# The last round of a fused attention and expert kernel: sums loaded and made earlier, a bias added by TensorE, a gate product made ahead, mixes put between the scores, and four stores of one tile each

## The reference, cut to what matters

```python
xn = layernorm(x)
q, k, v = (xn @ W + b).reshape(b, s, 4, 256)        # 4 heads
scores = (q*cos . k*cos + q*sin . k*sin) / 16        # [b, s, head, head] at every position
out = softmax(scores) @ v                            # mixes the 4 heads of one position
s_ = swapaxes(out, 1, 2).reshape(b, s, 4*256) @ Wo + bo
# experts: 8, two of them for every position, gates from a Sinkhorn router
e = sum over the 2 chosen of gate * ((relu(xn @ wg) * (xn @ wp)) @ wo)
result = x + s_ * silu(xn + e)
```

## Time and profile before

| | |
|---|---|
| median of 3 runs | 1723.53 us (1723.3 to 1725.36) |
| the profiled execution's own time | 1719.48 us |
| its span | 1717.7 us |
| TensorE busy | 95% of the span |
| GpSimd busy | 46% of the span |
| mean granted TensorE clock | 0.985 of full |

### The profile page before, as it was taken

The page is one execution under the profiler, slowest core; times in us unless marked ns, Lnnn a source line. Parts: engine busy times, 40 slices in busy tenths (PEclk is TensorE's granted clock), DMA queues, the critical chain, the costliest instruction groups (busy, mean ns, idle before and its releaser), DMA issues.

```text
span 1717.7 us, 28581 instructions
## 1 busy us (share of the span) xinstructions
PE 1638.2 (95%) x9328; PEld 1271.6 (74%) x9328; DVE 994.2 (58%) x1895; ACT 734.5 (43%) x1207; POOL 792.1 (46%) x961
## 2 busy tenths in 40 slices
PE   4899899989999999999999999999999999999994
PEld 2446766678888888888888887776687767877663
DVE  6567889853333333333333335667777677776775
ACT  3666333413333333333333335345554455543551
POOL 4665378713433333343434432525545455452435
PEclk9999999999999999999999999999999999999997
DMA  9997633163313131313111412444546445455234
GB/s 332 401 360 245 248 123 104 51 249 127 126 53 124 56 123 56 124 55 123 56 56 56 153 54 85 152 138 160 169 154 214 137 159 171 154 178 172 91 122 131
DMA packets 161574, 250.96 MB, mean 146 GB/s; under 512 B 13864, under 2 KB 121184, under 8 KB 160288
## 3 DMA queue, kind: packets, MB, share of 16 engines
q1 hardware_dynamic: 147968, 213.57, 35.8%
q0 software_dynamic: 12960, 35.41, 6.3%
q10 hardware_dynamic: 512, 0.16, 0.0%
HBM read 149.58 MB, written 99.50 MB: 145 GB/s over the span
## 4 chain that ended last, share of the span: by engine, by line
PE 84%; DMA 5%; DVE 4%; SPq 2%; ACT 2%; POOL 2%; issue 1%; ACTq 0%; POOLq 0%; DVEq 0%
PE ps L1075 20%; PE ps L1012 20%; PE ps L1023 13%; PE ps L967 12%; PE ps L1094 10%; PE ps L1084 3%; DMA AUX<-xn_d,AUX 3%; PE ps L981 2%; PE ps L1057 2%; DVE UN L1159 1%; PE ps L922 1%; PE ps L866 1%; SPq L323 1%; DMA WR<-w_d 1%; SPq L304 1%
## 5 line engine op out<-in xcount | busy, mean ns | idle before, releaser
L1075 PE MATMUL ps<-WR,FR 128*128 x1620 | 409.8, 402 | 5.2 <-issue 2.7
L1075 PEld LDWEIGHTS ps<-WR,FR 128*128 128x128 f32 x1620 | 297.5, 190 | 64.6 <-issue 6.8
L603 POOL DMA_INDIRECT y_d<-AUX x135 | 133.3, 987 | 368.2 <-ACT AUX L810 368.2
L1574 DVE TENSOR_TENSOR AUX<-AUX,ps 128x512 f32<-128x512 f32 x135 | 92.9, 688 | 348.2 <-ACT AUX L798 348.2
L760 ACT ACTIVATE WM<-ps,bcs,trig 128x512 f32<-128x512 f32 x256 | 255.7, 1019 | 90.2 <-PE ps L1012 82.4
L1510 DVE TENSOR_SCALAR WM<-ps,vec,trig 128x512 f32<-128x512 f32 x256 | 246.4, 995 | 63.9 <-ACT WM L760 63.5
L967 PEld LDWEIGHTS ps<-WM 128*128 128x128 f32 x2048 | 230.6, 192 | 9.0 <-issue 5.8
L1023 PE MATMUL ps<-WM,XTJ 128*128 128x512 f32 x512 | 237.1, 600 | 0.0
L967 PE MATMUL ps<-WM 128*128 128x128 f32 x2048 | 234.6, 276 | 2.0 <-DVE TM L1406 2.0
L798 ACT ACTIVATE AUX<-ps 128x512 f32<-128x512 f32 x135 | 80.9, 599 | 324.5 <-PE ps L1075 324.5
L1012 PE MATMUL ps<-XH,WH 128*128 128x512 f32 x512 | 205.1, 401 | 6.5 <-issue 5.5
(11 more groups left out here) (234 smaller groups left out, 2218.9 us busy)
## 6 DMA issues: line engine op xcount, KB each, us to landing
u_d<-UN SPq DMA_DIRECT2D x128, 256.0 KB, 2.0
US<-u_d SPq DMA_DIRECT2D x64, 512.0 KB, 4.7
WR<-w_d SPq DMA_DIRECT2D x8, 3072.0 KB, 10.9
AUX<-y_d SPq DMA_DIRECT2D x30, 512.0 KB, 5.9
WM<-in_L_attn_x_dram SPq DMA_DIRECT2D x16, 512.0 KB, 9.3
xn_d<-WM SPq DMA_DIRECT2D x32, 256.0 KB, 8.7
w_d<-WH SPq DMA_DIRECT2D x16, 512.0 KB, 8.4
w_d<-WL SPq DMA_DIRECT2D x16, 512.0 KB, 9.4
```

Of the source, the lines that this page charges most:

```text
L603: e.indirect_dma_start(y_d, bass.IndirectOffsetOnAxis(toks[:, m - 5:m - 4], 0), YS[:, (m - 5) % 2, :], None).then_inc(s_y[(m - 5) % 2], 16)
L1075: mm = e.matmul(b[:, :], x, WR[:, bass.ds(off[m] + (2048 * z + 1024 * a + 512 * k), 512)], start=(k == 0 and x is xh and z == 0), stop=(k ...
L1574: e.tensor_tensor(HS[:, m % 2, :], GR[:, :], mP[m % 2][:, :], ALU.mult).then_inc(s_h, 1)
```

## The change

- `load_c(15)` is issued at the end of round 14's part of the SyncE queue, right behind `load_c(14)`, into other tiles (cE1 to cE3, which the totals of rounds 0 to 3 used, and AB for x), with a semaphore of its own. The U of item 63 goes to XB and waits for no mix.
- On GpSimd `total(15)` stands ahead of `finish(14)`. ScalarE's `silu(15)` stands behind group 23 of round 15. A new function `ahead` on GpSimd, behind `finish(14)`, makes gate times bo (into xn's tile) and adds x to it (4 x 2 operations).
- The mix of items 60 to 63 no longer waits for VectorE's bias: TensorE adds BR with four more matmuls a mix. `mixed` of these items makes `PSUM * gate` and then adds what `ahead` made, and so takes in `result`.
- Mix 60 stands behind the scores of item 62, mix 61 behind the scores of item 63; on VectorE each item's spread stands behind the next item's soft_a.
- `store_last` stores each item with one DMA as soon as it is ready.

```diff
@@ cs, us
-            return [M_s[:, i // 2, 2048 * (i % 2):2048 * (i % 2) + 1024].rearrange("p (i d) -> p i d", d=D)
-                    for i in range(4)]
+            return cE1, cE2, cE3, AB[:, :, :].rearrange("p a (i d) -> p (a i) d", d=D)
+        ends = cs(NQ - 1)
+        def us(n):
+            return XB[:, :, :] if n == 4 * NQ - 1 else US[:, n % 3, :, :]
@@ SyncE
+            def store_last(n):
+
+                e.wait_ge(s_rl, n - 4 * NQ + 5)
+                e.dma_start(rows(of, NQ - 1)[:, :, n % 4, :].rearrange("h r d -> r h d"),
+                            cs(NQ - 1)[3][:, n % 4, :]).then_inc(s_o, 16)
@@ SyncE, segment
+                    if q == NQ - 2:
+                        e.wait_ge(s_es, 64 * QE)
+                        load_c(NQ - 1)
                 if q1 == NQ:
-                    e.wait_ge(s_ch, 24 * NQ)
-                    load_c(NQ - 1)
                     load_u(4 * NQ - 1)
...
-            store_c(NQ - 1)
+            for n in range(4 * NQ - 4, 4 * NQ):
+                store_last(n)
@@ GpSimd
+            def ahead():
+
+                _, y2, xn, xx = cs(NQ - 1)
+                e.wait_ge(s_cg, NQ - QE)
+                for i in range(4):
+                    ch(e.tensor_tensor(xn[:, i, :], y2[:, i, :], bo_b[:, :], ALU.mult))
+                    e.tensor_tensor(xx[:, i, :], xn[:, i, :], xx[:, i, :], ALU.add).then_inc(s_z, 1)
...
-                if q > QE:
+                if QE < q < NQ:
                     total(q - 1)
                 if q in host:
                     total(host[q])
-                if q > QE:
+                if q == NQ - 1:
+                    total(q)
+                if QE < q < NQ:
                     finish(q - 1)
+                if q == NQ - 1:
+                    ahead()
@@ ScalarE, segment
+                        if q == NQ - 1 and c == 23:
+                            silu(q)
...
-                if q1 == NQ:
-                    silu(NQ - 1)
@@ TensorE, mix
                 for c in range(4):
-                    mm = e.matmul(pM(n)[32 * c:32 * c + 32, :],
-                                  AT[:, n % 2, 32 * c:32 * c + 32], US[:, n % 3, c, :], start=True, stop=True)
+                    at = AT[:, n % 2, 32 * c:32 * c + 32]
+                    last = n < 4 * NQ - 4
+                    mm = e.matmul(pM(n)[32 * c:32 * c + 32, :], at, us(n)[:, c, :], start=True, stop=last)
+                    if not last:
+                        mm = e.matmul(pM(n)[32 * c:32 * c + 32, :], at, BR[:, :], start=False, stop=True)
@@ VectorE, mixed
+                i = n % 4
+                _, y2, _, xx = ends
+                e.wait_ge(s_z, i + 1)
+                e.tensor_tensor(ro(n), pM(n), y2[:, i, :], ALU.mult).then_inc(s_pm, 1)
+                e.wait_ge(s_pm, n + 1)
+                e.tensor_tensor(xx[:, i, :], ro(n), xx[:, i, :], ALU.add).then_inc(s_rl, 1)
@@ VectorE, segment
                         if i:
                             soft_b(n - 1)
+                        if q == NQ - 1 and i:
+                            spread(n - 1)
+                            if i == 3:
+                                mixed(n - 3)
...
-                spread(n)
-                biased(n)
-                spread(n + 1)
-                biased(n + 1)
-                for i in range(4):
-                    mixed(n + i)
-                    if i < 2:
-                        spread(n + i + 2)
-                        biased(n + i + 2)
+                if q1 == NQ:
+                    spread(4 * NQ - 1)
+                    for i in range(1, 4):
+                        mixed(4 * NQ - 4 + i)
```

More of the change, by code:

```diff
@@ L226, in program @@
         s_o = sem("s_o")
-        s_sa2, s_pm = sem("s_sa2"), sem("s_pm")
+        s_sa2, s_pm, s_u63, s_c15, s_z, s_rl = (
+            sem(n) for n in ("s_sa2", "s_pm", "s_u63", "s_c15", "s_z", "s_rl"))
         block = ctx.enter_context(nc.Block())
@@ L365, in load_u @@
                     e.wait_ge(s_uw[i], 16 * ((w - i + 2) // 3))
-                if n >= 3:
+                if n == 4 * NQ - 1:
+                    e.wait_ge(s_xt, 2 * NQ)
+                elif n >= 3:
                     e.wait_ge(s_mx, n - 2)
-                e.dma_start(US[:, n % 3, :, :], u_in[n]).then_inc(s_us[n % 3], 16)
+                e.dma_start(us(n), u_in[n]).then_inc(s_u63 if n == 4 * NQ - 1 else s_us[n % 3], 16)
             def store_r(n):
@@ L379, in store_c @@
                     e.dma_start(rows(of, q)[h], cs(q)[3][h:128:4]).then_inc(s_o, 16)
+            def store_last(n):
+                e.wait_ge(s_rl, n - 4 * NQ + 5)
+                e.dma_start(rows(of, NQ - 1)[:, :, n % 4, :].rearrange("h r d -> r h d"),
+                            cs(NQ - 1)[3][:, n % 4, :]).then_inc(s_o, 16)
             def load_c(q):
                 y1, y2, xn, xx = cs(q)
-                e.dma_start(y1, blk(y_d, q)).then_inc(s_cl, 16)
-                e.dma_start(y2, blk(y_d[N:2 * N, :], q)).then_inc(s_cl, 16)
-                e.dma_start(xn, blk(xn_d, q)).then_inc(s_cl, 16)
+                sl = s_cl if q < NQ - 1 else s_c15
+                e.dma_start(y1, blk(y_d, q)).then_inc(sl, 16)
+                e.dma_start(y2, blk(y_d[N:2 * N, :], q)).then_inc(sl, 16)
+                e.dma_start(xn, blk(xn_d, q)).then_inc(sl, 16)
                 if QE < q < NQ - 1:
@@ L389, in load_c @@
                 for h in range(H):
-                    e.dma_start(xx[h:128:4], rows(xf, q)[h]).then_inc(s_cl, 16)
+                    e.dma_start(xx[h:128:4], rows(xf, q)[h]).then_inc(sl, 16)
             def load_e(k):
@@ L610, in total @@
                 else:
-                    e.wait_ge(s_cl, 112 * (q - QE + 1))
+                    e.wait_ge(*((s_cl, 112 * (q - QE + 1)) if q < NQ - 1 else (s_c15, 112)))
                     y1, y2, xn, _ = cs(q)
@@ L974, in mix @@
                 e.wait_ge(s_atc, n + 1)
-                e.wait_ge(s_ub, n + 1)
+                if n < 4 * NQ - 4:
+                    e.wait_ge(s_ub, n + 1)
+                elif n == 4 * NQ - 1:
+                    e.wait_ge(s_u63, 16)
+                else:
+                    e.wait_ge(s_us[n % 3], 16 * (n // 3 + 1))
                 if n == 0:
@@ L1039, in segment @@
                         scores(4 * q + i)
+                        if q == NQ - 1 and i >= 2:
+                            mix(4 * q + i - 2)
                         place(lists.get((q, 24 + i), ()))
                 if q1 == NQ:
-                    for i in range(4):
-                        mix(4 * q1 - 4 + i)
+                    mix(4 * NQ - 2)
+                    mix(4 * NQ - 1)
             e.wait_ge(s_wsp, 4)
@@ L1453, in mixed @@
                     e.wait_ge(s_ro, n - 4 * QE - 3)
-                e.tensor_tensor(ro(n), pM(n), bo_b[:, :], ALU.add).then_inc(s_pm, 1)
+                if n < 4 * NQ - 4:
+                    e.tensor_tensor(ro(n), pM(n), bo_b[:, :], ALU.add).then_inc(s_pm, 1)
+                    return
+                i = n % 4
[4 more added lines that the diff above has]
+                e.tensor_tensor(xx[:, i, :], ro(n), xx[:, i, :], ALU.add).then_inc(s_rl, 1)
             def early(k):
@@ L1537, in segment @@
                     soft_b(4 * q + 3)
-                if q1 == QE:
-                    return
-                n = 4 * q1 - 4
-                spread(n)
-                biased(n)
-                spread(n + 1)
-                biased(n + 1)
-                for i in range(4):
-                    mixed(n + i)
-                    if i < 2:
-                        spread(n + i + 2)
-                        biased(n + i + 2)
+                if q1 == NQ:
+                    spread(4 * NQ - 1)
+                    for i in range(1, 4):
+                        mixed(4 * NQ - 4 + i)
             segment(0, QE)
```

## The result

The changed kernel took 1713.41 us in the median of 11 runs (1707.27 to 1718.27), the kernel before 1723.53 (1719.94 to 1728.47, 11 runs). The ratio is 0.9925, with a 95% interval of 0.9909 to 0.9942: faster by 0.75%, 10 to 16 us. That ratio is not the quotient of the two medians: they lie 10.1 us apart (0.9941), at the low end of the interval. Its profiled execution took 1709.11 us with a span of 1707.4, so 10.3 us less span than before.

A forecast was written before the change was run, and what follows sets the result against it. TensorE bounds the rounds; behind the last scores, 27.3 us of load, GpSimd total, silu, result and store. Leaving VectorE's chain and mixes there cuts the span from 1717.7 to 1704.4, giving a 1710.2 us median, range 1708.6 to 1714.5.

The forecast's parts named there:

- What bounds the end: Behind the scores: 27.3 us on load, GpSimd's total, silu, result, store; VectorE's chain ends only 4.5 us earlier.
- The early load and total cost nothing: Rounds 14 and 15: load lands about 1651, second total ends about 1663, TensorE's rounds stay at 53.7 us.
- a rival of up to 1 us: Ahead of mix 56: moved totals slow VectorE, TensorE waits up to 1 us; chance 0.55 together with the forecast.
- `ahead` and silu 15 hidden: Round 15: silu fits ScalarE's 4.30 us wait; GpSimd's product ends at 1684.0, first read at 1695.7.
- The price of a mix with a bias: Mixes 60 to 63 on TensorE: 1.14 us at full clock taken, against 0.57 without bias.
- The low bound: Mixes with bias: column groups run side by side, 1.14 us of TensorE; VectorE starts after 1.17, or 2.06 at half clock.
- the middle price: Mixes with bias: groups hold each other up, about 2.0 us, or 4.0 at half clock; chance 0.38.
- The sum: Behind round 15's scores: VectorE's chain, mix 63 and last store end the span at 1704.4 against 1717.7, 13.3 us less.
- The clock: At mix 63: TensorE granted half clock after little work, so 2.06 us; at full clock 0.8 us less.
- rival 1: Mixes 60 to 63 take about 2.0 us, or 4.0 at half clock: time 1711.2 to 1714.8 us; chance 0.38.

The follow-up runs named there:

- early-only run: Kernel before with only round 15's early load, total and silu; bias, results and four stores unchanged: 75.4 us from round 15's start to the end, against 80.2.
- kept-busy version: Changed kernel plus eight, then four, unread matmuls behind mixes 61 and 62: 68.2, then 66.1 us from round 15's start to the end, against 66.9.
- late operation: Changed kernel plus one unread GpSimd multiplication waiting for the last addition: 69.8 us from round 15's start to the end, against 66.9.

## Why the prediction was right

- **What bounds the end.** Right, and the early-only run shows it: with GpSimd's total off the path the tail fell by 4.8 us, not by 13.3. VectorE was next. It is chance, though, that 4.8 lies near the 4.5 us by which VectorE's chain had ended ahead of GpSimd's: of that lead only 2.7 us could be had, since VectorE's last result still had to go through GpSimd, and the other 2.1 us came from VectorE's operations, which GpSimd's total had stretched. The sum had this right without saying it: it took VectorE's operations at their usual length.
- **The early load and total cost nothing.** Right but for 0 to 0.5 us. The second total ended 24 us behind the start of round 15 in the first profile (25.7 in round 9, my model), and 27.7 in the second, where TensorE waited 0.45 us ahead of mix 56. That was in the text as a rival of up to 1 us.
- **`ahead` and silu 15 hidden.** Right: `ahead` ended at 1687.0 and was first needed at 1698.7, silu 15 stood in ScalarE's wait. VectorE's two-input operation beside GpSimd in soft_a 60 took 0.34 us in place of 0.17, with 1.58 us of waiting behind it.
- **The price of a mix with a bias.** The low bound held and was 0.12 us too high: 1.02 us of TensorE's time at full clock against 1.14 taken (0.57 for one without a bias), and VectorE starting 2.03 us behind mix 63 at half clock against 2.06. The four column groups run side by side although U and BR of one group stand back to back. The Trainium skill's rule (TensorEngine Tiling (Array Packing), Tiling Modes, Key Properties) that tiles work in parallel agrees with these rows, and the middle price, which a strict order of issue would give, is out.
- **The sum.** Predicted from the start of round 15: scores 63 at 50.7 us, measured 50.6; mix 63 at 61.5, measured 61.4; the tail 66.9, measured 66.9 and 67.3. One term held only by what the sum left out: 2.55 us from the last store to the end needs GpSimd's last operation to start at least 2.6 us before that store (5.1 less 2.5). It did, at 1686.27 against 1704.9, but the prediction did not ask for it.
- **The clock.** Mix 63 at half clock, as taken, in both profiles; mix 62 was at half in the first and at full in the second, and VectorE waited for it in neither. The rows of the kept-busy version price mix 63 at 0.8 us.
- **What was off.** The median, 1713.4 against 1710.2: the head of the program varies by 8 us from one execution to the next, more than the 0.8 us that I gave to the difference between two medians. That the range held the median was in part luck: its upper end was meant for rival 1. A second comparison, of 4 and 7 runs, had medians of 1711.26 and 1724.2, 12.9 us apart. The ratio, also 12.9 us, with an interval of 10.0 to 15.7, holds the 13.3 predicted.

The gain of 13.3 us is made up so, by one order of taking parts away: early load, total and silu 4.8 us; bias on TensorE, results taken into mixed with the product made ahead, and a store for each item, together 7.3 us (75.4 to 68.1), of which the bias is worth 2.2 and the stores 2.1 when each is undone alone; spreads and mixes between the scores 1.3 us, which is 2.7 gained on VectorE less 1.4 lost because mix 60 holds the last scores up. Each piece can be off by the 0.5 us by which tails vary. The value of the product made ahead was not tried alone, nor was that of the earlier load of item 63's U.

## What to carry to other kernels

Ahead of a move that takes the longest chain off the end, measure the second longest: it caps the gain, here at 4.8 of 13.3 us. Look also at what the two chains' engines do to each other: 2.1 of the 4.8 came from VectorE's operations, which were shorter once GpSimd was idle beside them. Work put into the gaps of an engine must not stand ahead of the operation that the bound engine waits for: mixes between the scores cost 1.4 us, spreads there gained 2.7. When a small gain at the end is sought in a program whose head varies, cut the span at a point that both versions share, and compare the granted clock ahead of it.

## What the runs showed of the hardware that was not expected

- The end of GpSimd's program is a bound of its own: its close ended 4.87 to 4.90 us behind the start of its last operation in fourteen profiles, and where that was the last thing to end, the span ended 5.1 us behind it (late operation: 1707.60 to 1712.7), against 2.5 us from the start of the last store to the end.
- Two matmuls in a row on the same 32 columns of the array did not slow the other column groups: 16 passes of 256 columns in 1.02 us at 2.4 GHz, where 8 took 0.57.
- The expert part of the same program took from 673 to 682 us in fourteen profiles, with 6.8 to 23.8 us of it at half clock; less half of that it is 668.3 to 670.7.
